# Audio tower on one core: areas for five experts, and adding scatters into the output for the last three

## What is computed

```python
logits = x_flat @ Wr                                  # 4096 x 8
probs = jax.nn.softmax(logits, axis=0)
vals, idx = jax.lax.top_k(probs.T, C)                 # 8 experts, C = 1024 tokens each
selected = x_flat[idx]
h = gelu(einsum('ecd,edf->ecf', selected, W1) + b1[:, None, :])    # 128 -> 512
out_e = einsum('ecf,efd->ecd', h, W2) + b2[:, None, :]             # 512 -> 128
weighted = vals[..., None] * out_e
output = zeros_like(x_flat).at[idx.reshape(-1)].add(weighted.reshape(-1, Dd))
```

## Time and profile before

| | |
|---|---|
| median of three runs | 902.28 us |
| the profiled execution, its own time | 906.52 us |
| its span, first to last instruction | 904.6 us |
| PE busy | 681.8 us (75%) |
| DVE busy | 606.8 us (67%) |
| ScalarE busy | 455.7 us (50%) |
| POOL busy | 172.6 us (19%) |
| DMA moved | 57.22 MB, mean 63 GB/s |
| mean granted clock of TensorE | 0.867 |

### The profile page before, as it was taken

How to read it: one execution, slowest core, us unless ns; L and a number is a source line. 1 busy time by engine, 2 the same in 40 slices (tenths; PEclk the granted TensorE clock), 3 DMA queues, 4 the chain that set the end, 5 groups by cost and what they waited for, 6 DMA issues and landing times.

```text
span 904.6 us, 12917 instructions
## 1 busy us (share of the span) xinstructions
PE 681.8 (75%) x4060; PEld 447.9 (50%) x4060; DVE 606.8 (67%) x2175; ACT 455.7 (50%) x664; POOL 172.6 (19%) x219
## 2 busy tenths in 40 slices
PE   4688679579999999999999986733155666856870
PEld 3254455365575765756757564422134344533650
DVE  2878887788979888788696898278764422441124
ACT  3968548348768776787777876320021210221210
POOL 1000000000010010100100000010076466456451
PEclk9799799789999999999999988855566889877995
DMA  7992000000000000000000000020011244664778
GB/s 243 319 326 94 1 1 1 1 3 12 2 12 4 1 14 1 1 13 1 13 2 2 12 1 14 5 61 0 0 45 41 58 89 113 149 150 107 163 161 293
DMA packets 30573, 57.22 MB, mean 63 GB/s; under 512 B 8600, under 2 KB 23402, under 8 KB 28340
## 3 DMA queue, kind: packets, MB, share of 16 engines
q1 hardware_dynamic: 24544, 35.19, 12.2%
q0 software_dynamic: 5728, 20.98, 10.3%
q10 hardware_dynamic: 212, 0.08, 0.0%
HBM read 45.75 MB, written 25.17 MB: 78 GB/s over the span
## 4 chain that ended last, share of the span: by engine, by line
DVE 32%; PE 32%; issue 9%; another core or an unknown queue 8%; ACT 7%; DVEq 5%; DMA 3%; POOL 2%; ACTq 1%; SPq 0%; POOLq 0%
PE ps L787 4%; DVE back L1128 4%; PE ps L832 3%; DVE top L1131 3%; PE ps L865 3%; PE ps L976 3%; PE ps L881 3%; DVE front L1446 3%; DVE top L1099 3%; PE ps L990 2%; PE ps L805 2%; PE ps L769 2%; PE ps L855 2%; PE ps L892 2%
## 5 line engine op out<-in xcount | busy, mean ns | idle before, releaser
L584 ACT ACTIVATE front<-ps 128x1024 f32<-128x1024 f32 x128 | 127.7, 1027 | 36.3 <-PE ps L832 12.3
L682 ACT ACTIVATE front<-front,minus_tau 128x256 f32<-128x256 f32 x256 | 108.6, 497 | 37.0 <-DVE minus_tau L1227 35.8
L584 ACT ACTIVATE back<-ps 128x1024 f32<-128x1024 f32 x72 | 73.7, 1023 | 78.0 <-PE ps L962 64.8
L584 ACT ACTIVATE back<-ps,back 128x1024 f32<-128x1024 f32 x32 | 35.0, 1112 | 150.4 <-remote 102.6
L976 PE MATMUL ps<-back 128*128 128x512 f32 x128 | 70.7, 707 | 41.1 <-ACT back L584 39.8
L865 PE MATMUL ps<-ident,front 128*128 128x128 f32 x512 | 76.6, 299 | 30.3 <-ACTq L684 21.7
L865 PEld LDWEIGHTS ps<-ident,front 128*128 128x128 f32 x512 | 64.8, 154 | 53.0 <-ACTq L684 31.9
L1505 DVE TENSOR_TENSOR ps<-ps,back 128x512 f32<-128x512 f32 x16 | 11.2, 700 | 115.8 <-remote 60.5
L486 POOL CROSS_LANE_REDUCE more_all<-more 128x1 int32<-128x1 f32 x32 | 11.5, 358 | 399.2 <-DVEq L1152 266.1
L534 POOL DMA_INDIRECT back<-rows,back x64 | 63.2, 987 | 93.4 <-issue 69.1
L556 POOL DMA_INDIRECT plane<-back x64 | 62.3, 974 | 54.6 <-DVEq L1512 37.6
(11 more groups left out here) (194 smaller groups left out, 1135.4 us busy)
## 6 DMA issues: line engine op xcount, KB each, us to landing
h<-plane POOLq DMA_DIRECT2D x6, 2048.0 KB
back<-in_L_ffn_W_dram SPq DMA_DIRECT2D x16, 256.0 KB
front<-in_x_dram SPq DMA_DIRECT2D x4, 750.0 KB, 5.6
plane<-hid SPq DMA_DIRECT2D x2, 1024.0 KB, 6.5
rows<-xn SPq DMA_DIRECT2D x8, 256.0 KB, 2.2
front<-plane SPq DMA_DIRECT2D x1, 2048.0 KB, 8.2
front<-plane SPq DMA_DIRECT2D x4, 512.0 KB, 5.5
out_dram<-h SPq DMA_DIRECT2D x4, 512.0 KB, 4.5
```

The lines of the kernel that those rows point to most:

```text
L584: a.activation(dst, ps[s][:, 0:cols], func, **kw).then_inc(sems[f"free{s}"], 1)
L682: a.activation(prob[n % 2][:, r, :], sc[n][:, r, :], ACT.Relu, bias=minus_tau[:, n // 2, n % 2 * 4 + r:n % 2 * 4 + r + 1])
```

## The change

Areas are kept for experts 0 to SE-1 = 4 only, so four copies are made at the start and not seven. `slots` gives, for experts 5 to 7, the token's own row (as in `gather_at`) in place of the row in an area. POOL's order up to `scatter(4)` stays, and so does the area add halfway through each scatter, but for the last one: area 4 is added to `h` only at the start of `add(5)`, when expert 4's rows have landed. SyncE waits until all five area adds are done (`acc` at 80) and stores all of `h` to the output in one DMA, `out_ok`. POOL waits for that, and then scatters the rows of expert 5 into the output itself with indirect DMAs that add (`compute_op=ALU.add`); experts 6 and 7 follow, each after the rows of the one before have landed. The weights of expert 7 are issued on SyncE's queue behind the store. The areas' loads, the DVE adds and the four stores at the end are gone, and DVE's loop over experts 4 to 7 is written out in straight code.

```diff
--- before.py
+++ after.py
@@ -153,6 +153,7 @@
     INNER = HEADS * DH
     E = w_r.shape[1]
     F = e_w1.shape[2]
+    SE = E - 3
     CAP = min(1024, NTOK)
     CT = CAP // P
     EPS = 1e-5
@@ -161,7 +162,7 @@
     LOWEST = -3.0e38
 
     rows2 = nc.dram_tensor("rows2", (NTOK, D), f32, kind="Internal").ap()
-    plane = [nc.dram_tensor(f"plane{e}", (NTOK, D), f32, kind="Internal").ap() for e in range(E)]
+    plane = [nc.dram_tensor(f"plane{e}", (NTOK, D), f32, kind="Internal").ap() for e in range(SE)]
 
     ctx = ExitStack()
     with ctx:
@@ -316,8 +317,6 @@
         slot_f = sb("slot_f", [P, CT])
         slot_w = cut([P, E, CT])
         slot_i = cut([P, E, CT], i32)
-        NZ = 2
-        z = [cut([P, NT, D]) for i in range(NZ)]
 
         cut = back()
         ew1 = [cut([P, F]) for i in range(2)]
@@ -345,8 +344,7 @@
                  "mx_in", "mx_ok", "ex_in", "ex_ok", "sm_in", "sm_ok", "pr_ok", "round_ok",
                  "rest_ok", "vals_ok", "cnt_in", "rk_in", "hot_ok", "hot_quarter",
                  "slots_ok", "ew_in0", "ew_in1", "xg_in0", "xg_in1", "xg_used", "y_ok", "out_half", "y_out0", "y_out1",
-                 "y_free", "ew_used", "hid_zero", "plane0_in", "planes_in", "acc", "issued", "z_in0", "z_used",
-                 "zq_in0", "zq_in1", "zq_in2", "zq_in3", "out_ok"]
+                 "y_free", "ew_used", "hid_zero", "plane0_in", "planes_in", "acc", "out_ok"]
         sems = {n: None if n.startswith("slot") and n[4:].isdigit() else ctx.enter_context(nc.semaphore(n))
                 for n in names}
         block = ctx.enter_context(nc.Block())
@@ -408,7 +406,7 @@
             sp.dma_start(wr[:, :], w_r).then_inc(sems["att_w_in"], 16)
 
             sp.wait_ge(sems["plane0_in"], 32)
-            for e in range(1, E):
+            for e in range(1, SE):
                 sp.dma_start(plane[e][:, :], plane[0][:, :]).then_inc(sems["planes_in"], 16)
 
             with sp.Fori(0, G) as t:
@@ -430,26 +428,14 @@
                              allow_slow_non_contiguous=True).then_inc(sems[f"ew_in{p}"], 16)
                 sp.dma_start(eb2[p][:, :], e_b2[e, :].partition_broadcast(P)).then_inc(sems[f"ew_in{p}"], 16)
 
-            def scattered(e):
-                sp.wait_ge(sems[f"y_out{e % 2}"], (e // 2 + 1) * (16 * CT))
-
-            for e in range(2):
+            for e in range(E - 1):
                 weights_in(e)
-            for e in range(2, E):
-                weights_in(e)
-            for e in range(E - 2, E):
-                scattered(e)
-                if e < E - 1:
-                    sp.dma_start(z[0][:, :, :], plane[e].rearrange("(p j) d -> p j d", p=P)).then_inc(sems["z_in0"], 16)
-            last = plane[E - 1].rearrange("(p j) d -> p j d", p=P)
-            for q in range(4):
-                rows = slice(q * NT // 4, (q + 1) * NT // 4)
-                sp.dma_start(z[1][:, rows, :], last[:, rows, :]).then_inc(sems[f"zq_in{q}"], 16)
-            for q in range(4):
-                rows = slice(q * NT // 4, (q + 1) * NT // 4)
-                sp.wait_ge(sems["z_used"], q + 2)
-                sp.dma_start(orow[:, rows, :], h[:, rows, :]).then_inc(sems["out_ok"], 16)
-            sp.wait_ge(sems["out_ok"], 64)
+            sp.wait_ge(sems["acc"], 16 * SE)
+            sp.dma_start(orow, h[:, :, :]).then_inc(sems["out_ok"], 16)
+            weights_in(E - 1)
+            for p in range(2):
+                sp.wait_ge(sems[f"y_out{p}"], ((E + 1 - p) // 2) * (16 * CT))
+            sp.wait_ge(sems["out_ok"], 16)
 
         @block.gpsimd
         def _(g):
@@ -535,6 +521,18 @@
                                          bass.IndirectOffsetOnAxis(ap=gather_at[p][:, s:s + 1], axis=0))\
                         .then_inc(sems[f"xg_in{p}"], 16)
 
+            def landed(e):
+                g.wait_ge(sems[f"y_out{e % 2}"], (e // 2 + 1) * (16 * CT))
+                g.sem_inc(sems["y_free"], 1)
+
+            def area_added(e):
+                if e > 0:
+                    g.wait_ge(sems["acc"], e * 16)
+                g.sem_inc(sems["pool_held"], 1)
+                g.dma_start(h[:, :, :].rearrange("p j d -> p (j d)"),
+                            plane[e].rearrange("(p j) d -> p (j d)", p=P), accum_op=ALU.add,
+                            max_dma_last_dim=8192).then_inc(sems["acc"], 16)
+
             def scatter(e):
                 p = e % 2
                 g.wait_ge(sems["y_ok"], e * 2 + 1)
@@ -542,32 +540,42 @@
                 for s in range(CT):
                     if s == CT // 2:
                         if e:
-                            g.wait_ge(sems[f"y_out{1 - p}"], ((e - 1) // 2 + 1) * (16 * CT))
-                            g.sem_inc(sems["y_free"], 1)
-                        if 0 < e < E - 1:
-                            if e > 1:
-                                g.wait_ge(sems["acc"], (e - 1) * 16)
-                                g.sem_inc(sems["pool_held"], 1)
-                            g.dma_start(h[:, :, :].rearrange("p j d -> p (j d)"),
-                                        plane[e - 1].rearrange("(p j) d -> p (j d)", p=P), accum_op=ALU.add,
-                                        max_dma_last_dim=8192).then_inc(sems["acc"], 16)
+                            landed(e - 1)
+                            area_added(e - 1)
                         g.wait_ge(sems["y_ok"], e * 2 + 2)
                         g.sem_inc(sems["pool_held"], 1)
                     g.indirect_dma_start(plane[e][:, :], bass.IndirectOffsetOnAxis(ap=add_at[p][:, s:s + 1], axis=0),
                                          y[p][:, s, :], None).then_inc(sems[f"y_out{p}"], 16)
 
+            token_row = out.rearrange("b s d -> (b s) d")
+
+            def add(e):
+                p = e % 2
+                if e == SE:
+                    landed(e - 1)
+                    area_added(e - 1)
+                    g.wait_ge(sems["out_ok"], 16)
+                else:
+                    landed(e - 1)
+                g.wait_ge(sems["y_ok"], e * 2 + 1)
+                g.sem_inc(sems["pool_held"], 1)
+                for s in range(CT):
+                    if s == CT // 2:
+                        g.wait_ge(sems["y_ok"], e * 2 + 2)
+                        g.sem_inc(sems["pool_held"], 1)
+                    g.indirect_dma_start(token_row[:, :], bass.IndirectOffsetOnAxis(ap=add_at[p][:, s:s + 1], axis=0),
+                                         y[p][:, s, :], None, compute_op=ALU.add).then_inc(sems[f"y_out{p}"], 16)
+
             g.sem_inc(sems["y_free"], 2)
             for e in range(4):
                 gather(e, e % 2)
-            g.wait_ge(sems["planes_in"], 16 * (E - 1))
-            for e in range(E - 5):
+            g.wait_ge(sems["planes_in"], 16 * (SE - 1))
+            for e in range(E - 4):
                 scatter(e)
                 gather(e + 4, e % 2)
-            scatter(E - 5)
-            gather(E - 1, 1)
-            for e in range(E - 4, E):
-                scatter(e)
-            g.engine_nop().then_inc(sems["issued"], 1)
+            scatter(SE - 1)
+            for e in range(SE, E):
+                add(e)
 
         @block.scalar
         def _(a):
@@ -1467,7 +1475,7 @@
                     v.drain().then_inc(sems["hot_quarter"], 1)
                 v.drain().then_inc(sems["hot_ok"], 1)
 
-            def slots(n, p, first=False):
+            def slots(n, p, first=False, in_area=True):
 
                 e = n * 2 + p
                 job = c.job(3)
@@ -1478,8 +1486,11 @@
                 v.scalar_tensor_tensor(gather_at[p][:, :], parts[:, 0, :], float(P), parts[:, 1, :], ALU.mult, ALU.add)
                 v.drain().then_inc(sems["slots_ok"], 1)
                 v.tensor_tensor(parts[:, 2, :], parts[:, 2, :], parts[:, 3, :], ALU.add)
-                v.scalar_tensor_tensor(slot_i[:, ds(e, 1), :].rearrange("p e s -> p (e s)"), parts[:, 1, :], float(NT),
-                                       parts[:, 0, :], ALU.mult, ALU.add)
+                if in_area:
+                    v.scalar_tensor_tensor(slot_i[:, ds(e, 1), :].rearrange("p e s -> p (e s)"), parts[:, 1, :],
+                                           float(NT), parts[:, 0, :], ALU.mult, ALU.add)
+                else:
+                    v.tensor_copy(slot_i[:, ds(e, 1), :].rearrange("p e s -> p (e s)"), gather_at[p][:, :])
                 v.drain()
                 v.tensor_tensor(slot_w[:, ds(e, 1), :].rearrange("p e s -> p (e s)"), parts[:, 2, :], parts[:, 4, :],
                                 ALU.add)
@@ -1519,30 +1530,13 @@
                 one_hots(2 + p)
                 slots(1, p)
             weighted(0, 0)
-            with v.Fori(0, (E - 4) // 2) as n:
-                c.enter(n, 0, {"slot3": 4})
-                for p in range(2):
-                    one_hots(n * 2 + (4 + p))
-                    slots(n + 2, p)
-                    weighted(n + p, 1 - p)
-                c.leave((E - 4) // 2)
+            for e in range(4, E):
+                one_hots(e)
```

(16 more changed lines are left out.)

## The result

The changed kernel takes 914.19 us (median of seven runs, 910.89 to 917.74), the kernel before 902.28 us (median of seven, 900.71 to 907.49): ratio 1.012 with the interval [1.0092, 1.0149], so 1.2% slower. The forecast was 898.4 us, with a range from 893.5 to 909.5. The profiled execution of the changed kernel took 915.21 us, and its span is 913.4 us; that of the kernel before had 906.52 and 904.6.

A forecast was written before the change was run, and what follows sets the result against it. It took POOL–DVE–POOL rounds to bound the expert loop and 14.6 us of transfers to follow the last scatter. Loop 1.8 us earlier, then area add, store and three 12.69 us experts: span 904.6 to 900.7, so 898.4 us, range 893.5 to 909.5.

The forecast's parts named there:

- half again as many entries: Upper bound on an adding scatter's extra POOL issue: half again as many entries cost half again 0.96, so 0.48 us.
- the full stretch of the earlier trace: Area 4 add: DMA nearly full from 849.26 to near 862.6, plus receipt, taken as 13.4 us from issue to landing.
- Rival 2: Adding scatters at the end: POOL issue proportional to entries, 1.44 us instead of 0.96, +9.1 us, 907.5; chance 0.17.
- Rival 3: Adding scatters at the end: DMA engines pay per row, a scatter needs 2.1 us, outlasting its issue; +18, 916; chance 0.07.
- Rival 1: Tail: landings stay at 3.85 us because writes to the output are slow; +3.9 us, 902.3, no visible gain; chance 0.13.
- the gather row: Landing with wake-up of a plain scatter, taken from expert 0's last gather issue to PE's start: 2.55 us.
- Rival 4: Expert loop: the written-out DVE loop brings nothing or runs into the hold; +1.8 us, 900.2; no separate chance given.
- start-up copies: Start of the kernel: removing three of seven area copies was claimed to be worth 0.
- weights of expert 7: SyncE's queue behind the store: landing 3 to 6 us after it, PE work still hidden with 2 to 8 us cover.

The follow-up runs named there:

- e7: The changed kernel with 64 of 128 rows left out of every scatter of experts 4 (plain) and 5 to 7 (adding): 909.98 us, one execution.
- e6: The kernel before with expert 7's eight scatters adding into their own zeroed area: 905.96 us against 903.14, ratio 1.0044.
- e10: The changed kernel with the last three experts' scatters writing and not adding, second measurement: 869.55 us, ratio 1.0072 to the kernel before.
- e12: The changed kernel itself, measured again at the lower level: 886.64 us, ratio 1.0258 to the kernel before.
- e3: The changed kernel with the last three experts' scatters writing and not adding, first measurement: 869.52 us, ratio 1.0058 to the kernel before.
- e9: The kernel before with only DVE's loop over experts 4 to 7 written out, at the lower level: 865.67 us, ratio 1.0013.
- e13: The kernel before with only DVE's loop over experts 4 to 7 written out, at the higher level: 903.6 us, ratio 0.9990.
- e8: The kernel before with DVE's loop written out, POOL's area adds removed, areas loaded by SyncE and added by DVE: 901.95 us, ratio 0.9983.

## Why the prediction was wrong

The sum, term by term, in the profiled execution:

| step | forecast | measured | difference |
|---|---|---|---|
| area 4 add issued | 840.3 | 835.18 | −5.1 |
| area add, issue to landing | 13.4 | 13.38 | 0 |
| store of h | 8.3 | 8.32 | 0 |
| first scatter after it | 0.1 | 1.8 | +1.7 |
| 21 steps from scatter to scatter | 21 x 1.363 = 28.6 | 13.15 + 13.05 + 13.05 = 39.25 | +10.6 |
| last issue to the next expert's first, twice | 6.3 | 5.16 + 4.22 = 9.4 | +3.1 |
| last issue to the end | 3.55 | 6.02 | +2.5 |
| end of the span | 900.7 | 913.4 | +12.7 |

- **The step that failed is the issue cost of an adding scatter.** It was taken as 0.10 us above a plain one, with 0.48 as the upper bound; it is 0.60, outside the bound. Put into the forecast's own sum, 24 x 0.50 us turn 898.4 into 910.4, which alone is past the range. The forecast drew the price from the area add L551, a DMA without indirect addresses, and turned its 0.40 us for 512 entries into a price per entry. e7's line puts 0.39 us on the instruction, which no division by entries can show, and the 0.21 us that go with the rows are twice the 0.10 taken; e6 shows that the price belongs to the adding form of the instruction. The upper bound was no measurement but a mechanism, "half again as many entries". With no row of such an instruction the range should have been kept wide: 24 x 0.5 us decide the sign.
- **Luck.** The terms that came out dearer add up to 17.9 us; a loop that ended earlier than forecast, for the most part by the spread between traces, hid 5.1 of them. The 13.4 us of the area add came out exact, but they are the full stretch of the earlier trace rows with 0.1 us left for the landing, where the store was given 2.3; that trace had scatters beside the add. That it came out exact is luck in part.
- **Rival 2 named the right place** (POOL paces the end, 1.44 us, 907.5), and its point of decision, 1.22 us, was passed. Its reason, cost in proportion to entries, explains 0.21 of the 0.60 us by e7's line. **Rival 3** is right in direction only: DMA is 0.37 busy in 860 to 872 with 1.86 us per scatter, 0.69 us of all engines for each, against 0.2 before and 2.1 in the rival. It stays below the issue time and so hidden. **Rival 1** is refuted: plain rows land in the output in 2.24 us (e10) and not in 3.85.
- **Landing and restart.** From the last issue of an expert to the first of the next the forecast had 2.55 us for plain rows and 0.6 more with the add (0.10 of issue, 0.5 of landing). With plain rows the step measured 3.13, so the base was 0.6 short: the gather row held PE's restart and not POOL's. With the add it was 5.16 and 4.22, that is 2.0 and 1.1 more, of which 0.60 are the longer issue. The 2.15 us that the forecast worked out as an estimate from the Trainium skill's "DMA: Bandwidth & Descriptors" (section "Anatomy of one DMA") is near the 2.24 us that plain rows take to land, but the sum needed the restart as well.
- **What was left out.** Between a landing and POOL's next scatter lie 0.88 us, and 1.85 us between the store's landing and the first scatter, 1.79 of them in one piece, in e10 too. The profile calls this time "issue" and does not show what POOL does in it. At the end SyncE waits 2.2 us for PE's program, 2.5 in e10 and 2.1 in e12, where it was 0.2 before; the forecast took 0.4 for all that follows the last landing. Why the end is longer when POOL has the last work is not shown.
- **Loop.** The area 4 add came 5.1 us before its forecast. The gather of expert 7 started 7.7 us earlier where 1.8 was forecast, which makes 5.9; 0.8 us are given back, 0.2 because expert 4's rows land a little later and 0.6 because POOL takes 0.67 us from there to the area add and not 0.1. The direct effect that was forecast is there in part: DVE's idle time ahead of the first instruction of the four `one_hots` (1.7 us in the earlier trace rows, L1449) is gone, but that ahead of L1458's place was 0.8 us and is 2.7. But in the table of traces most of the 5.9 is spread: medians and not single traces make the loop's share 16.5 − (914.19 − 902.28) = 4.6 us. Forecast 1.8, bounds 0 to 3.7. Rival 4, that the loop brings nothing, holds at the lower level and is not excluded at the higher.
- **Would it have been faster with plain scatters?** By this estimate, no; at the higher level no such kernel was run. The tail from 858.75 with e3's 38.28 us would end at 897.0, 93.2 us after the gather of expert 7. The kernel before needs 92.7. At the lower level e10 needs 91.9 against 84.9. Part of the reason can be seen: the forecast had the area 4 add go out 9 us earlier. Counted from the gather of expert 7 it goes out 6.4 us earlier at the higher level (31.3 against 37.7 us), but only 0.8 us at the lower (30.4 in e10, 31.2 in e9), and that is most of why the change costs more there. Behind it one queue runs area add, store and three experts, each waiting for the one before, and that takes as long as what it replaced or longer.
- The hidden parts held: start-up copies, weights of expert 7, PE, DVE and ScalarE at the end. PE started on expert 7 at 858.7, 1.8 us after the store's landing where 3 to 6 were taken, and both halves were weighed by 879.7 and not at 883 to 889; the 3 us that the forecast guessed for a fallen clock show in no run.

No version run here beats the kernel before by more than can be measured; e13 and e8 lie 0.1% and 0.2% below it, inside their intervals.

## What to carry to other kernels

A DMA that adds by indirect addresses must be priced as an instruction of its own: measure one, in place, before the end of a kernel is built on 24 of them in a row. Edits that replace wide transfers by chains of small DMAs trade DMA time for an engine's issue time; count issues, landings and restarts on the one queue, and compare them with the old end's waits, not with its busy time. And a single trace of a loop that waits for unnamed signals can be 4 us off: split the span at a fixed instruction and compare the parts over several traces.

## What the runs showed of the hardware

- An adding indirect scatter of 128 rows of 512 bytes occupies POOL for 1.56 us, a plain one for 0.96, whether it writes to the output or to an area; with 64 rows 1.40 and 0.90 (e7).
- The last adding scatter of an expert lands 3.2 to 4.7 us after it starts (seven traces), a plain one 2.24 (e3, e10).
- POOL starts its next scatter 0.88 us after such a landing, and 1.85 us after the landing of SyncE's store.
- POOL's indirect DMA issue, started during a 4.4 to 4.5 us DVE add of two SBUF tiles, took 4.07 to 5.18 us in all six places of e8 and ended 0.8 to 0.9 us after DVE.
- The same program came out at 864 and at 902 to 907 us in different comparisons, on one chip too. Three rounds of the loop (gathers of expert 4 to 7) take 67 us at the lower level (704.55 to 771.49 in e9) and 88 us at the higher (723.15 to 811.56 in the kernel before), where DVE and ScalarE wait for signals the profile doesn't name.
